# Decays of three linear-attention stages in PSUM, their sums by channel, and DMA issue and filler matmuls of the softmax attention moved

## Time and profile before

| | us |
|---|---|
| median of 3 runs | 1269.7 (1269.53 to 1271.92) |
| the profiled execution | 1268.4 |
| its span | 1266.7 |
| softmax attention from the first maxima | about 54 to 502 |
| scans of the gated stage | 551.9 to 635.8 |
| scans of the retention stage | 682.1 to 763.4 |
| scans of the lightning stage | 978.4 to 1059.2 |

### The profile page before, as it was taken

The page is one execution under the profiler, slowest core; times in us unless marked ns, Lnnn a source line. Parts: engine busy times, 40 slices in busy tenths (PEclk is TensorE's granted clock), DMA queues, the critical chain, the costliest instruction groups (busy, mean ns, idle before and its releaser), DMA issues. The chain is left out here.

```text
span 1266.7 us, 17452 instructions
## 1 busy us (share of the span) xinstructions
PE 989.5 (78%) x5892; PEld 500.1 (39%) x5892; DVE 873.5 (69%) x1502; ACT 511.3 (40%) x1048; POOL 479.7 (38%) x506
## 2 busy tenths in 40 slices
PE   5477899899999999686767775399984985369994
PEld 3222222222222333544453223166661544236663
DVE  6957889898988830889878985633337997643335
ACT  5234577687877776320021101033334321113333
POOL 2311110011101112248834883146642797136662
PEclk9657889899999999789868986599996997679997
DMA  6881000000000000511001101011112110101114
GB/s 134 175 192 19 1 1 1 1 1 2 1 1 1 2 3 7 193 58 51 9 1 33 51 17 33 13 32 42 43 37 75 59 34 1 34 21 42 43 43 116
DMA packets 50204, 51.45 MB, mean 41 GB/s; under 512 B 7668, under 2 KB 39804, under 8 KB 50108
## 3 DMA queue, kind: packets, MB, share of 16 engines
q1 hardware_dynamic: 44888, 40.06, 12.4%
q0 software_dynamic: 4992, 10.23, 3.0%
q10 hardware_dynamic: 240, 0.05, 0.0%
HBM read 33.22 MB, written 16.91 MB: 40 GB/s over the span
## 5 line engine op out<-in xcount | busy, mean ns | idle before, releaser
L720 DVE TENSOR_REDUCE mpart<-ps 128x2 f32<-128x1024 f32 (+3 forms) x320 | 325.3, 1061 | 59.4 <-PE ps L771 34.2
L841 ACT ACTIVATE arena<-ps 128x512 f32<-128x512 f32 (+3 forms) x640 | 292.1, 542 | 143.2 <-PE ps L788 133.9
L788 PE MATMUL ps<-arena 51*128 51x512 bf16 (+3 forms) x640 | 182.3, 372 | 14.9 <-ACT arena L841 6.2
L1085 POOL TENSOR_TENSOR arena<-arena 128x512 f32<-128x512 f32 x96 | 148.6, 1559 | 64.9 <-DVE arena L1134 63.7
L771 PE MATMUL ps<-arena 51*128 51x512 bf16 (+3 forms) x640 | 149.9, 383 | 21.2 <-DVE mpart L720 15.7
L802 PE MATMUL ps<-arena,w 128*32 128x512 f32 (+3 forms) x1280 | 160.5, 575 | 2.9 <-ACT arena L841 2.5
L690 POOL TENSOR_SCALAR_AFFINE_SELECT arena<-arena 128x512 f32<-128x512 f32 x64 | 40.6, 634 | 313.8 <-ACT arena L841 231.3
L1669 ACT ACTIVATE arena<-ps 128x512 f32<-128x512 f32 x78 | 46.6, 597 | 219.6 <-PE ps L1732 163.4
L1579 DVE COPY arena<-ps 128x128 f32<-128x128 f32 x78 | 22.8, 292 | 154.4 <-PE ps L1722 146.5
L1134 DVE TENSOR_TENSOR_SCAN arena<-cst,arena 128x512 f32<-128x512 f32 x64 | 124.0, 1959 | 2.0 <-POOL arena L1090 2.0
L788 PEld LDWEIGHTS ps<-arena 51*128 51x128 bf16 x640 | 50.2, 95 | 174.5 <-ACT arena L841 136.4
(11 more groups left out here) (263 smaller groups left out, 1525.6 us busy)
## 6 DMA issues: line engine op xcount, KB each, us to landing
w<-in_w SPq DMA_DIRECT2D x2, 2048.0 KB, 11.4
arena<-results SPq DMA_DIRECT2D x16, 256.0 KB, 4.9
arena<-q_stack SPq DMA_DIRECT2D x8, 384.0 KB
arena<-k_stack SPq DMA_DIRECT2D x8, 384.0 KB
arena<-g_v SPq DMA_DIRECT2D x9, 256.0 KB
arena<-r_v SPq DMA_DIRECT2D x9, 256.0 KB, 3.6
arena<-l_v SPq DMA_DIRECT2D x9, 256.0 KB, 3.6
tokens<-arena SPq DMA_DIRECT2D x8, 256.0 KB, 2.4
```

The costliest lines, as they stand in the source:

```text
L720: nc.vector.tensor_reduce(out=mpart[:, 2 * pl:2 * pl + 2, t, kc], in_=ps[:, bank:bank + 2, 0:width], axis=AX.X, op=ALU.max).then_inc(ring_ ...
L788: nc.tensor.matmul(ps[:, n % ST, off:CH], rows(Ks, j % 2, 2 * g + j // 2, kt * P, (kt + 1) * P), rows(Qs, j % 2, 2 * g + j // 2, c * CH + ...
L841: nc.scalar.activation(probs[:, n % 2, j[0], off:CH], ps[:, (GH * n + j[0]) % ST, off:CH], ACT.Exp, scale=float(HD) ** -0.5).then_inc(exp_ ...
L1085: nc.gpsimd.tensor_tensor(z[:, n % ZB, :], state[:, n % SB, :], q[:, c % 2, :], ALU.mult).then_inc(z_ready, 1)
```

## The change

For the linear stages:

- The decay lies in PSUM. For gated, ACT writes it in place over the key projection, whose bank alternates between 2 and 0 (`decay_bank`). For the others DVE copies the constant column to `ps[:, 0, 0:1]` once and repeats that.
- The sum over e is one matmul of 128 x 512 per z for all three kinds, by channels.
- New `outer(c)` on PE, at e = 6 of the next chunk: gated projects the four tiles of the copied sum with `ho`, lightning turns them. It waits for ACT's `copy_inner` (at e = 4). Lightning then has a second ACT copy, `copy_outer`, at e = 7.
- gated's add moves from after scan 5 to after scan 7, lightning's statistics from scan 6 to scan 7.
- The values for DRAM use bank 1 instead of 0, the layer norm banks 1 and 7 instead of 0 and 1. `orep` and its 8 DMAs go.

For attention: SP issues all of `set_maxima`, with `store` and `stack` of chunks 2 and 3 behind those of steps 1 and 3, each behind a wait for that step's DMAs; and the planner may put fills in the next score bank too.

```diff
-                while can[what][0] - pe > 0.25 and free <= pe:
+                n = GH * su + sj
+                bank_free = n < GH * NU and (n < 3 or exp_end[n - 3] + 0.06 <= pe) if n < 3 or len(exp_end) > n - 3 else False
+                while can[what][0] - pe > 0.25 and (free <= pe or bank_free):
...
-                    plan.append(("fill", slots))
+                    plan.append(("fill", slots) if free <= pe else ("fill scores", n))
...
-                        for c in (2, 3):
-                            store(sp, c)
-                            stack(sp, c)
-                        for k in range(EARLY, NS):
+                        for k in range(NS):
                             set_maxima(sp, k)
+                            if k in (1, 3):
+                                c = (k + 3) // 2
+                                for j in range(GH):
+                                    sp.wait_ge(max_set[j], 16 * (k + 1))
+                                store(sp, c)
+                                stack(sp, c)
...
+                        def fill_scores(n):
+                            if n >= ST:
+                                pe.wait_ge(exp_done, n - ST + 1)
+                            nc.tensor.matmul(ps[:, n % ST, 0:320], identb[:], cstb[:, 0:320], start=True, stop=True)
...
-                            if what == "turn max" and n < EARLY:
-                                set_maxima(act, n)
...
+                    if kind != "gated":
+                        column = C_RET if kind == "retention" else C_LT
+                        nc.vector.tensor_copy(ps[:, 0, 0:1], cst[:, column:column + 1]).then_inc(decay_set, 1)
+                        dve.wait_ge(decay_set, 1)
...
-                        a = dec[:, c % 2, :] if kind == "gated" else \
-                            cst[:, C_RET if kind == "retention" else C_LT:][:, 0:1].to_broadcast([P, CH])
+                        a = ps[:, decay_bank[c % 2], :] if kind == "gated" else ps[:, 0, 0:1].to_broadcast([P, CH])
...
-                        if kind == "gated" and c >= 1 and n % HD == LAG + 1:
+                        if kind == "gated" and c >= 1 and n % HD == HD - 1:
                             add(dve, c - 1)
-                        if kind != "gated" and c >= 1 and n % HD == LAG + 2:
+                        if kind != "gated" and c >= 1 and n % HD == (LAG + 2 if kind == "retention" else HD - 1):
                             y_statistics(dve, c - 1)
...
-                def copy_out(act, c):
+                def copy_inner(act, c):
                     act.wait_ge(z_used, (c + 1) * HD)
+                    if kind == "retention":
+                        nc.scalar.copy(y[:, c * CH:(c + 1) * CH], ps[:, 6 + c % 2, :]).then_inc(sum_out, 1)
+                    else:
+                        if c >= 2:
+                            act.wait_ge(outer_ready, c - 1)
+                        nc.scalar.copy(inner[:, c % 2, :], ps[:, 6 + c % 2, :]).then_inc(inner_out, 1)
+
+                def copy_outer(act, c):
+                    act.wait_ge(outer_ready, c + 1)
                     nc.scalar.copy(y[:, c * CH:(c + 1) * CH], ps[:, 6 + c % 2, :]).then_inc(sum_out, 1)
...
-                            nc.scalar.activation(dec[:, c % 2, :], pk, ACT.Sigmoid, bias=col["key_b"])
...
-                            nc.scalar.activation(k[:, c % 2, :], pk, ACT.Sigmoid, bias=negb, scale=-1.0).then_inc(kq_out, 1)
+                            nc.scalar.activation(k[:, c % 2, :], pk, ACT.Sigmoid, bias=negb, scale=-1.0)
+                            nc.scalar.activation(pk, pk, ACT.Sigmoid, bias=col["key_b"]).then_inc(kq_out, 1)
...
-                        if kind == "retention":
-                            ins = nc.tensor.matmul(ps[:, 6 + c % 2, :], reduce_w[:, e, :], z[:, n % ZB, :],
-                                                   start=e == 0, stop=e == HD - 1)
-                        else:
-
-                            for t in range(TPC):
-                                ins = nc.tensor.matmul(ps[:, 6 + c % 2, t * P:(t + 1) * P], z[:, n % ZB, t * P:(t + 1) * P],
-                                                       reduce_w[:, e, :], start=(e, t) == (0, 0), stop=(e, t) == (HD - 1, TPC - 1))
-                        ins.then_inc(z_used, 1)
+                        nc.tensor.matmul(ps[:, 6 + c % 2, :], pick[:, e, :], z[:, n % ZB, :], start=e == 0,
+                                         stop=e == HD - 1).then_inc(z_used, 1)
+
+                    def outer(c):
+
+                        pe.wait_ge(inner_out, c + 1)
+                        for t in range(TPC):
+                            out, tile = ps[:, 6 + c % 2, t * P:(t + 1) * P], inner[:, c % 2, t * P:(t + 1) * P]
+                            if kind == "gated":
+                                ins = nc.tensor.matmul(out, tile, w["ho"][:], start=True, stop=True)
+                            else:
+                                ins = nc.tensor.transpose(out, tile, ident)
+                        ins.then_inc(outer_ready, 1)
```

More of the change, by code:

```diff
@@ L814, in _ @@
                                 fill(n)
+                            if what == "fill scores":
+                                fill_scores(n)
                             if what == "max":
@@ L1018, in linear_attention @@
             vrep = take(HD * P).rearrange("p (e h d) -> p e h d", e=HD, h=H)
-            orep = take(HD * P).rearrange("p (e m) -> p e m", e=HD)
+            inner = take(2 * CH).rearrange("p (b t) -> p b t", b=2)
             y = take(T)
@@ L1025, in linear_attention @@
             UB = 4
-            upd = [half[:, i * CH:(i + 1) * CH] for half in (upd, low_rank if kind == "gated" else spare) for i in (0, 1)]
+            upd = [half[:, i * CH:(i + 1) * CH] for half in (upd, spare) for i in (0, 1)]
             negb = take(1)
@@ L1039, in linear_attention @@
             v_loaded = [sem(f"{name}_v_loaded{b}") for b in range(VB)]
-            norm = Norm(name, x, xn, NT, 1e-5)
+            norm = Norm(name, x, xn, NT, 1e-5, banks=(1, 7))
+            decay_set = sem(name + "_decay_set")
+            decay_bank = (2, 0) if kind == "gated" else (0, 0)
             rep_ready = sem(name + "_rep_ready")
@@ L1057, in linear_attention @@
             gate_out = sem(name + "_gate_out")
-            orep_loaded = sem(name + "_orep_loaded")
-            if kind == "gated":
-                reduce_w = orep
-            else:
-                reduce_w = pick
+            inner_out = sem(name + "_inner_out")
+            outer_ready = sem(name + "_outer_ready")
             def wait_update(eng, n):
@@ L1093, in add @@
                     x_statistics(dve, x_added, c - 1)
-                    dve.wait_ge(z_used, (c + 1) * HD)
+                    dve.wait_ge(outer_ready, c + 1)
                     xs = x[:, c * TPC:(c + 1) * TPC, :]
@@ L1197, in _ @@
                             nc.scalar.copy(gate[:, c * CH:(c + 1) * CH], ps[:, 1, :]).then_inc(gate_out, 1)
-                        if e == LAG and c >= 1 and kind != "gated":
-                            copy_out(act, c - 1)
+                        if e == LAG and c >= 1:
+                            copy_inner(act, c - 1)
                         if e == LAG + 1 and c + 1 < NC:
                             take_kq(c + 1)
-                    if kind != "gated":
-                        copy_out(act, NC - 1)
+                        if e == HD - 1 and c >= 1 and kind == "lightning":
+                            copy_outer(act, c - 1)
+                    copy_inner(act, NC - 1)
+                    if kind == "lightning":
+                        copy_outer(act, NC - 1)
                 @block.tensor
@@ L1212, in project_kq @@
                                 pe.wait_ge(kq_out, 2 * c - 1 + j)
-                            nc.tensor.matmul(ps[:, 2 + j, :], w[weight][:], xT[:, o], start=True, stop=True).then_inc(kq_ready, 1)
+                            if c >= 2 and kind == "gated" and j == 0:
+                                pe.wait_ge(scanned, (c - 1) * HD)
+                            bank = decay_bank[c % 2] if kind == "gated" and j == 0 else 2 + j
+                            nc.tensor.matmul(ps[:, bank, :], w[weight][:], xT[:, o], start=True, stop=True).then_inc(kq_ready, 1)
                     def add_product(n):
@@ L1249, in _ @@
                                 pe.wait_ge(v_full_out, c)
-                            nc.tensor.matmul(ps[:, 0, :], w[wv][:], xT[:, (c + 1) * CH:(c + 2) * CH],
+                                if kind == "lightning":
+                                    pe.wait_ge(gate_out, c)
+                            nc.tensor.matmul(ps[:, 1, :], w[wv][:], xT[:, (c + 1) * CH:(c + 2) * CH],
                                              start=True, stop=True).then_inc(v_full_ready, 1)
@@ L1253, in _ @@
                             pe.wait_ge(norm.out, NC)
+                            pe.wait_ge(v_full_out, min(c + 1, NC - 1))
                             if c >= 1:
@@ L1263, in _ @@
```

(8 more changed lines are left out.)

9 lines of the change are left out of this document (2 added, 7 removed).

## The result

| | before | changed |
|---|---|---|
| median of the runs, us | 1269.6 (1267.28 to 1271.92) | 1185.2 (1181.0 to 1186.4) |
| profiled execution, us | 1268.4 | 1181.0 |
| its span, us | 1266.7 | 1179.3 |
| three scan stretches together, us | 246.1 | 178.9 |
| first scan of the gated stage | 551.9 | 532.4 |

The ratio is 0.9329, with a 95% interval of 0.9301 to 0.9358: 84.4 us less. The forecast was 1206, the range 1184 to 1236. The time lies inside it, at its lower end. The profiled execution is the fastest of the four.

The account below looks back on a forecast made before the run. No engine bounds the whole; in the scan stretches DVE's scan and POOL's multiply largely exclude one another. 1268.4 - 51.7 (linear stages) - 12 (attention) = 1204.7 us profiled, 1206 for the median; range 1184 to 1236.

Parts of the forecast that it names:

- The scan: Linear stages: with its decay in PSUM, DVE's scan takes 1.21 us instead of a median of 1.92.
- C: Rival, linear stages: the scan isn't freed and stays at 1.92 us; time 1261, chance 0.07.
- E: Rival, linear stages: the PSUM operand slows the scan itself, to 2.30 us; time 1298, chance 0.02.
- POOL: Linear stages: POOL's multiplies, at most 2.19 us before, go to 1.25 us.
- The work sums: Scan stretches from work at PE's full clock: gated 59.4, retention 54.9, lightning 60.7, sum 175.0 us, 71.1 less.
- The handover loss: Linear stages: time lost in handovers between engines, 12% on the nine chunks after chunk 0, 15.9 us.
- The clock (B): Rival, linear stages: PE's clock becomes the bound, staying at 0.84; time 1225, chance 0.17.
- Given back, 3.5 us: Linear stages: gated's end costs 1.7 us more, lightning's 1.3, copying the decay column some 0.25 twice.
- The attention: Attention: moved issues and fills together bring 12 us.
- The queue's -8: Attention: ACT no longer issues set_maxima; about 3 us each for steps 1 and 3, 2 for step 0.
- The fills' -4: Attention: 108 score fills, placed in estimated gaps, may raise PE's clock; -4 us taken between -18 and +33.
- D: Rival, attention: the fills cost what they occupy on PE, +33 us for -4; time 1243, chance 0.08.

Follow-up runs that it names:

- e5: The changed kernel with the decays back in SBUF, sums by channel and attention staying as changed: 1255.8 us.
- e7: The changed kernel with each value projection of the linear stages issued twice on PE: 1229.0 us.
- e2: The changed attention joined to the linear stages of the kernel before: 1254.3 us, 17.5 less than the kernel before.
- e4: The kernel before with only the new planner's score-bank fills, ACT still issuing set_maxima of steps 0 to 3: 1257.6 us.
- e1: The changed linear stages joined to the attention of the kernel before: 1203.7 us, 68.1 less than the kernel before.
- e11: The changed kernel run once more, unedited, in a later batch: 1185.7 us.
- e3: The kernel before with only the moved issues (SP issues all of set_maxima), no fills in the score banks: 1258.1 us.
- e10: The changed kernel with key and query projections one step later and a fourth value channel by DMA in chunks 1 to 3: 1181.4 us.

## Why the prediction was right, and where its sizes were off

**The scan.** Predicted 1.21, measured 1.21 alone and 1.26 in the median; this step of the mechanism came out as worked out, and `e5` shows it as the cause. For the scan with POOL idle the two places of the decay give at least 1214 ns (SBUF, `e5`) and 1211 (PSUM). VectorE: DVE Perf Modes of the Trainium skill, "The TRN2 errata", has in its table 62 cycles more for a PSUM source, and says itself that the table's SBUF figure is too low; these rows show no such difference, and nothing of its 6 us came. Rivals C and E are refuted by the same row. One word in PSUM read 512 times (retention, lightning) costs the same as 512 words (gated): 1.21 at least and 1.26 in the median in all three stages.

**POOL.** Predicted 1.25, measured 1.27. What is still held is DVE's add with two SBUF inputs: 1.52 us while POOL multiplies until 594.80, and then 0.69 alone. DVE at gated's end, in the changed kernel:

```profile
592.36 0.85 DVE L194 BATCH_NORM_STATS2 stats<-x 128x6 f32<-128x128 f32 x4
593.13 0.68 DVE L1105 TENSOR_TENSOR x<-ps,x 128x512 f32<-128x512 f32 x1
593.84 1.52 DVE L1107 TENSOR_TENSOR x<-x,out_bias 128x512 f32<-128x512 f32 x1
595.39 0.87 DVE L194 BATCH_NORM_STATS2 stats<-x 128x6 f32<-128x128 f32 x4
597.85 0.69 DVE L1105 TENSOR_TENSOR x<-ps,x 128x512 f32<-128x512 f32 x1 [1.59 <-PE ps L1257]
598.58 0.69 DVE L1107 TENSOR_TENSOR x<-x,out_bias 128x512 f32<-128x512 f32 x1
```

**The work sums.** Predicted 59.4, 54.9 and 60.7, sum 175.0; measured 60.0, 56.2 and 62.7, sum 178.9. These held.

**The handover loss** is the term that failed: "I put 12% on the nine chunks after chunk 0 (132.8 us): 15.9". Measured is 178.9 - 175.0 = 3.9, that is 3%. The 12% came from chunks of the kernel before, where POOL was late by up to 3.15 us and PE worked at the lower clock in the chunk behind it. Both were results of the held scan: they left with it, and in `e5` the stretches came back with it (244.2). The loss of a list was read off a state that the change removes.

**The clock (B).** Predicted near 1.00 with a chance of 0.17 for 0.84; it is 1.00 in all three stretches. `e5` shows the direction: with the decay back in SBUF alone it falls to 0.90 and 0.92, so the clock followed the waits and was not a bound by itself. `e7` rules the bound out from the other side: more work on PE, same clock.

**Given back, 3.5 us.** At gated's end the last scan's end to the first of the last adds (597.85) takes 5.4 us, where it took 4.7: +0.7 and not +1.7. `outer` hides beside the adds of the chunk before. At lightning's end 5.5 against 5.3. The copy of the decay column, 0.15 us, stands 3 us ahead of the first update's values, which DVE waits for anyhow: nothing. So the two ends cost 0.9 us. With what lies between and behind the stages, the pieces outside the stretches come to -0.7, 4.2 below this term. The pieces behind gated's end are within the spread: from retention's last to lightning's first scan the three profiles of the same linear stages take 213.3, 214.0 and 214.1 us, and behind lightning's last 208.1, 209.2 and 207.3.

**The attention.** Predicted -12, measured -19.5 in the profile and -17.5 in `e2`'s runs. The queue's -8 was -11.5 by itself. The fills' -4 was -12.0 by itself, and D, which had +33 for it, is refuted by `e4`. The trace did carry the missing part: the clock of 0.50 was read the earlier trace rows and its worth bounded (-18), but the value taken leaned on neither end. Four windows of the kernel before run at 0.50, 0.61, 0.66 and 0.83 (as in `e1`), the same four after at 0.74, 0.67, 1.00 and 1.00. `e1` has PE busy for 13.1, 15.5, 15.8 and 16.6 us in them. The same work at the new clocks would take 8.9, 14.1, 10.4 and 13.8, that is 13.8 less in all (an estimate, by the ratio of the clocks; with those of the repeat `e11`, 0.81, 1.00, 0.74 and 1.00, it is 15.5). The copy of step 4's maxima came 13.0 earlier (155.6 to 142.6). So PE's clock is enough to account for most of the gain; how much of it the shorter waits give by themselves wasn't separated.

Two signs that I named have to be read with care. The first exponential is at 68.94, 1.1 sooner and not 2; in the other kernels with the changed attention it comes between 67.7 and 69.3, so the 2 is within the spread. And a stack DMA is waited for, but not at step 4: it is `stack(1)`, at step 2. ACT and PE of the changed kernel, then SP:

```profile
65.82 0.58 PE L819 MATMUL ps<-cstb,identb 128*128 128x320 bf16 x3
67.95 0.39 PE L775 MATMUL ps<-arena 51*128 51x512 bf16 x2 [1.55 <-DMA arena<-k_stack]
68.94 3.60 ACT L852 ACTIVATE arena<-ps 128x512 f32<-128x512 f32 x8 [18.68 <-PE ps L792]
...
64.07 13.17 SPq L660 DMA_DIRECT2D arena<-mrow  x8
78.39 3.90 SPq L377 DMA_DIRECT2D q_stack<-w  x6
82.33 3.86 SPq L377 DMA_DIRECT2D k_stack<-w  x6
```

PE reaches the maxima of step 2 before the chunk has landed, and holds 1.55 us there. That is not a result of the change: `e1` and `e3` hold 2.7 us at the same place, the first with the attention of before, while neither the kernel before nor `e4` nor any of the other eight profiles with this same attention waits there at all. SP's list, by contrast, is as worked out: `store(2)` starts at 78.4, near the 80 predicted, and nobody waits for it. ACT has no idle time on "issue" before 130, as predicted.

**The sum.** The forecast for a profiled execution was 1204.7 and 1181.0 was measured. The 23.7 between them are 12.0 of handover loss, 7.5 of attention (5.5 by `e2`'s runs, the rest being an early profile) and 4.2 of what was thought given back. All three err to the same side, so nothing cancelled. The first two have one fault: waits and a clock of the old state were carried into the new one. The median stands 4.2 above the profiled execution instead of the 1.3 assumed, hence 1185.2.

What stays open: whether PE or DVE sets the gated and retention stages of the changed kernel, what limits once PE is relieved (`e10`), and how the attention's gain divides between clock and waits.

## What to carry to other kernels

Where a DVE instruction and GpSimd multiply side by side, look at the spread of one instruction's duration (min against median) and at which of its operands lie where; if a constant or an activation's output can be put into PSUM, the two engines can run side by side at nearly full rate (here 1.26 us in the median for a scan that needs 1.21 alone). When such a hold goes, work the stages out anew from durations alone, and don't carry over a loss in per cent that was read from stalled chunks. Two edits that each raise PE's clock in the same stretch need not add up: here the second brought about half of its 12 us. The clock of one window in one execution is a weak witness, so compare it over several profiles of the same code.

## What the runs showed that I had not expected

- Fills that occupy 24 us of PE cost nothing net and bring 12 us: they stand where the planner expects PE to wait, and the granted clock of the first window is 0.74 with them and 0.50 without. 53 more of them bring nothing.
- Two engines that exclude one another don't do so fully: 1.92 us for a scan that needs 1.21 and starts 0.43 into a multiply of 1.26, where a full wait of 0.83 would give 2.04. Whether the 0.12 us is the scan's own start-up or work beside each other isn't shown.
- DMA issues cost their queue's engine 0.65 (12 of `store(2)` in 7.8 us) to 0.9 us (4 on ACT in 3.65 us in `e4`) each.
